# A linear-attention and FFN layer on one core: TensorE visits later code, and the first batch is rearranged

## The reference

```python
x = x + attn(layernorm(x))                      # x: 32 x 512 x 256, float32
x = x + ffn(layernorm(x))                       # ffn adds its own input and a second layernorm
# attn: 16 heads of 16 features, phi = elu + 1, chunks of 128 rows, causal inside a chunk
q, k, v = phi(x @ Wq.T + bq), phi(x @ Wk.T + bk), x @ Wv.T + bv
scores = where(tril, q @ k.T, 0)
num = scores @ v + q @ S                        # S: sum of k.T @ v over earlier chunks
den = sum(q * (cumsum(k) + z))                  # z: sum of k over earlier chunks
attn = (num / den) @ Wo.T + bo
# ffn: both weights come as integers, minus 128, times a scale per group of 128 rows
ffn = x + 0.5 * (silu((layernorm(x) * gamma + beta) @ w1 + b1) @ w2 + b2)
```

## Time and profile before

| | us |
|---|---|
| median of 3 runs (lowest, highest) | 1394.21 (1392.43, 1395.14) |
| the profiled execution: time, span | 1391.56, 1389.8 |
| TensorE busy (weight load) | 1362.6 (1227.8) |
| VectorE, ScalarE, GpSimd busy | 1188.4, 1072.2, 659.1 |
| TensorE's share of the chain that ended last | 94% |

### The profile page before, as it was taken

One profiled execution on the slowest core, in us unless ns is written; L12 is line 12 of the kernel. 1 busy time (PEld: TensorE's weight loads), 2 busy tenths in 40 slices (PEclk: granted clock), 3 DMA queues, 4 the chain that ended last, 5 costly groups with the idle time before them and its releaser, 6 DMA issues.

```text
span 1389.8 us, 60917 instructions
## 1 busy us (share of the span) xinstructions
PE 1362.6 (98%) x25658; PEld 1227.8 (88%) x25658; DVE 1188.4 (86%) x1954; ACT 1072.2 (77%) x1754; POOL 659.1 (47%) x506
## 2 busy tenths in 40 slices
PE   6889999999999999999999999999999999999998
PEld 5778899988999988999988999888999889999887
DVE  7778888889888888888889888889888898888876
ACT  4668778888778887778887778887788887788863
POOL 3354443545444545444544445544535454445454
PEclk9899999999999999999999999999999999999999
DMA  6121211222211122212212212212112212112110
GB/s 180 43 48 45 60 41 50 53 53 45 60 38 53 45 57 48 59 36 55 45 45 60 47 45 58 45 45 60 43 48 53 53 45 60 39 51 49 42 31 31
DMA packets 93525, 71.89 MB, mean 52 GB/s; under 512 B 8768, under 2 KB 92992, under 8 KB 93504
## 3 DMA queue, kind: packets, MB, share of 16 engines
q1 hardware_dynamic: 92144, 71.59, 20.8%
q10 hardware_dynamic: 1360, 0.01, 0.1%
HBM read 38.03 MB, written 16.78 MB: 39 GB/s over the span
## 4 chain that ended last, share of the span: by engine, by line
PE 94%; DVE 2%; ACT 1%; issue 1%; DMA 1%; POOL 0%; SPq 0%; POOLq 0%; DVEq 0%; ACTq 0%
PE sc L308 25%; PE ring L308 19%; PE num L479 7%; PE num L308 6%; PE sc L449 5%; PE sc L370 5%; PE sc L371 5%; PE num L493 4%; PE ring L370 4%; PE ring L371 3%; PE ring L462 2%; PE num L352 2%; PE ring L435 2%; PE sc L343 1%; PE num L371 1%; PE num L370 1%
## 5 line engine op out<-in xcount | busy, mean ns | idle before, releaser
L1151 POOL TENSOR_TENSOR s_lo<-silu_f,s_hi 128x512 fp32r<-128x512 f32 x252 | 325.2, 1295 | 454.4 <-ACT s_hi L960 454.2
L953 ACT ACTIVATE silu_f<-silu_f 128x512 f32<-128x512 f32 x252 | 157.8, 626 | 28.1 <-DVE silu_f L691 27.2
L699 DVE TENSOR_TENSOR probs<-sc,causal 128x1024 f32<-128x1024 f32 x128 | 150.7, 1218 | 15.4 <-PE sc L449 12.5
L960 ACT ACTIVATE s_hi<-silu_f 128x512 fp32r<-128x512 f32 x252 | 153.7, 621 | 1.3
L1179 POOL TENSOR_TENSOR ln_rstd<-ln_in,minus_half 128x8 f32<-128x8 f32 x32 | 52.6, 1644 | 189.8 <-DVE ln_in L792 189.8
L308 PE MATMUL sc<-w_hi,s_hi 128*128 128x256 f32 x488 | 137.2, 281 | 0.0
L308 PE MATMUL sc<-w_hi,s_lo 128*128 128x256 f32 x488 | 137.1, 281 | 0.0
L308 PE MATMUL sc<-w_lo,s_hi 128*128 128x256 f32 x488 | 137.1, 281 | 0.0
L946 ACT ACTIVATE silu_f<-ring,bias,scale 128x512 f32<-128x512 f32 x93 | 72.4, 779 | 83.3 <-PE ring L371 79.3
L308 PE MATMUL ring<-w_lo,s_hi 128*128 128x256 f32 x480 | 134.9, 281 | 0.0
L308 PE MATMUL ring<-w_hi,s_lo 128*128 128x256 f32 x480 | 134.9, 281 | 0.0
(11 more groups left out here) (198 smaller groups left out, 4320.0 us busy)
## 6 DMA issues: line engine op xcount, KB each, us to landing
x_in<-in_x SPq DMA_DIRECT2D x32, 512.0 KB, 5.0
xb<-in_x SPq DMA_DIRECT2D x32, 512.0 KB, 3.4
rb<-den_rows SPq DMA_DIRECT2D x256, 64.0 KB
out<-out_t SPq DMA_DIRECT2D x64, 256.0 KB, 2.2
probs<-in_q SPq DMA_DIRECT2D x2, 512.0 KB, 8.8
silu_f<-in_q SPq DMA_DIRECT2D x2, 512.0 KB, 7.6
res<-in_sc SPq DMA_DIRECT2D x1, 512.0 KB, 7.4
out_t<-in_sc SPq DMA_DIRECT2D x1, 512.0 KB, 9.0
```

The lines of the kernel that those rows point to most:

```text
L699: masked.done(e.tensor_tensor(probs[:, t, 2 * h:2 * h + 2, :, :, :].rearrange("p g m a q -> p (g m a) q"), sc[:, 2 * h:2 * h + 2, :].rearr ...
L953: silu.done(e.activation(slot(j, A), slot(j, A), ACT.Silu))
L960: sh.done(e.activation(s_hi[:, j, :], slot(j, A), ACT.Copy))
L1151: sl.done(e.tensor_tensor(s_lo[:, j, :], slot(j, A), s_hi[:, j, :].bitcast(F32), ALU.subtract))
```

## The change

TensorE gets four landings, places that hold one empty instruction and a jump back. `visit` jumps to one and comes back; `landing_here` places it inside other code, which jumps over it. `values_landing` (between `values(0)` and `values(1)`) and `states_landing` (between `from_states(0)` and `from_states(1)`) are in the first batch and visited from the preparation. `second_landing` (behind `fc1(3)`) and `third_landing` (behind `fc1(6)`) are in the loop and visited from the first batch. The loop itself never visits them.

Around them, in preparation and first batch: the values' projection of batch 0 goes to banks 0 and 1, `w_q` is made by GpSimd, VectorE takes the statistics of the next input ahead of the features, the reciprocals come behind the second mask and `x_hat` behind the fourth, the small vectors for beta and their sum are placed elsewhere, with their products in the bank of `den`, the cumulations come ahead of `bias_1` and `x_hat`, and `q_by_parity` for batch 1 goes from ScalarE to GpSimd.

```diff
-        SPARE = 0
+        SPARE = (0, 1)
...
+        def v_bank(n, i):
+            return bank(SPARE[n]) if isinstance(i, int) and i < 0 else use_bank(f"v{n}")
...
-                            if (0 <= w.i + shift < B) if earlier else other in present:
+                            if earlier and w.i + shift == 0 and other in ("v0", "v1"):
+                                pass
+                            elif (0 <= w.i + shift < B) if earlier else other in present:
                                 takers.append((k, event, shift))
                                 break
                         else:
...
                     n += 1
             return last
-        def pe_tokens(e, w, n, lhs, use, present, event):
-            free_bank(w, use, present)
+        def pe_tokens(e, n, lhs, use, target, event):
             for h in range(2):
                 toks = slice((2 * int(use[-1]) + h) * P, (2 * int(use[-1]) + h + 1) * P)
-                last = pe_split3(e, use_bank(use)[:, h * D:(h + 1) * D], [
+                last = pe_split3(e, target[:, h * D:(h + 1) * D], [
                     ((lhs[0][:, t, toks], lhs[1][:, t, toks]), (w_hi[n][:, t, :], w_lo[n][:, t, :])) for t in range(T)])
             event.done(last)
+        outside = {}
+        def visit(e, landing):
+            e.br(landing)
+            outside[landing] = nc.switch_bb(f"{landing}_back").parent
+        def landing_here(e, landing):
+            e.br(f"{landing}_over")
+            with nc.body(landing, parent=outside[landing], valid_engines=[e.engine]):
+                e.nop()
+                e.br(f"{landing}_back")
+            nc.switch_bb(f"{landing}_over")
         def pe_iteration(e, i, A, Fn, N, N2, preparation=None):
             w = Waiter(e, i)
...
+                visit(e, "values_landing")
                 for c in range(C):
                     if c < C - 1:
                         e.wait_ge(p_xhat, c + 1)
...
+                pe_tokens(e, "v", (xt_hi, xt_lo), f"v{n}", v_bank(n, i), v_pe)
             def output_projection(n):
                 w.need(at_l)
-                pe_tokens(e, w, "o", attention_parts(N), f"wo{n}", present, wo_pe)
+                free_bank(w, f"wo{n}", present)
+                pe_tokens(e, "o", attention_parts(N), f"wo{n}", use_bank(f"wo{n}"), wo_pe)
             if not A and N:
                 first_transposes()
...
                     project_kq(n)
+                visit(e, "states_landing")
                 preparation["v"]()
+                preparation["values"]()
                 project_v(0)
                 project_v(1)
                 return
...
+                landing_here(e, "values_landing")
                 values(1)
                 x_transposes(0)
                 x_transposes(1)
                 from_states(0)
+                landing_here(e, "states_landing")
                 from_states(1)
                 project_kq(0)
                 project_kq(1)
                 project_kq(2)
+                visit(e, "second_landing")
                 preparation["o"]()
                 output_projection(0)
                 output_projection(1)
                 project_kq(3)
                 project_v(0)
                 project_v(1)
-                w.need(e_x1, 0, 0)
+                visit(e, "third_landing")
+                w.need(phi, 1, 0)
                 preparation["bias_1"]()
                 return
             if not A:
...
             values(0)
             fc1(2)
             fc1(3)
+            landing_here(e, "second_landing")
             fc1(4)
             values(1)
             from_states(0)
             x_transposes(1)
             fc1(5)
             fc1(6)
+            landing_here(e, "third_landing")
             fc1(7)
             with e.If(i != B - 1):
...
+                ve_norm_x(e, w, 2)
                 features(0)
                 features(1)
                 cumulate(0)
                 features(2)
                 features(3)
                 cumulate(1)
-                preparation["w1"]()
-                ve_norm_x(e, w, 2)
                 return
             if A and not Fn:
                 mask(*MASK_ORDER[0])
+                mask(*MASK_ORDER[1])
                 reciprocals()
-                mask(*MASK_ORDER[1])
-                ve_x_hat(e, w, 1)
+                preparation["w1"]()
                 mask(*MASK_ORDER[2])
                 mask(*MASK_ORDER[3])
+                ve_x_hat(e, w, 1)
                 sum_states()
-                preparation["biases"]()
+                preparation["parts"]()
                 input_lo(0)
                 input_lo(1)
                 preparation["o"]()
                 add_residual(1)
                 norm_x1()
                 ve_norm_x(e, w, 2)
+                preparation["beta"]()
                 norm_factors()
                 features(2)
                 features(3)
+                cumulate(0)
+                cumulate(1)
                 preparation["bias_1"]()
                 ve_x_hat(e, w, 2)
-                cumulate(0)
-                cumulate(1)
                 return
             if not A:
                 ffn_input_lo(0)
...
+                        v_bank(n, i)[toks, :].rearrange("p (c a x) -> p c a x", a=2, x=HD), ACT.Copy)
                 v_sb.done(last)
             def ffn_norm():
                 preparation["w2"]()
                 exponential(3)
                 values_out(0)
+                values_out(1)
                 ffn_norm()
-                values_out(1)
-                q_by_parity(0)
                 table_silu()
-                q_by_parity(1)
                 return
             if not N:
                 ffn_input_hi(0)
...
+                w.need(phi, 1, 2 * t + 1)
+                w.need(sc_pe, 0, t)
+                for odd in range(2):
+                    last = e.tensor_scalar(q_mask[:, t, odd, :], phi_q[:, t, :], parity[:, odd:odd + 1], None, ALU.mult)
+                q_par.done(last)
             def ln2_factors():
                 if not A:
                     return
             if A and not Fn:
                 input_bias()
+                q_by_parity(0)
                 ln2_factors()
                 po_norm(e, w, 2)
+                q_by_parity(1)
                 query_sums(0)
                 query_sums(1)
                 preparation()
         block = ctx.enter_context(nc.Block())
         WORDER = "kqvo"
-        V_QK, V_BIAS_O, V_W1, V_PARTS, V_W2, V_BETA = 2, 3, 4, 7, 8, 10
+        V_QK, V_BIAS_O, V_PARTS, V_W2, V_BETA = 2, 3, 5, 7, 9
         PAR = 6
         def stage_of(n):
...
+            for t in range(T):
+                e.tensor_scalar(w1_q[:, t, :], w1_i[t], -128.0, None, ALU.add).then_inc(p_w1, 1)
+            po_norm(e, Waiter(e, -1), 2)
             po_iteration(e, -1, False, False, True, False)
-            po_norm(e, Waiter(e, -1), 2)
             e.wait_ge(p_v, V_BIAS_O)
             def weights_2_lo():
...
-                e.wait_ge(p_wdma["1"], 16 * T)
-                for t in range(T):
-                    last = e.tensor_scalar(w1_q[:, t, :], w1_i[t], -128.0, None, ALU.add)
-                last.then_inc(p_v, 1)
-                e.wait_ge(p_v, V_W1)
-            def biases():
-                e.wait_ge(p_late, 16 * 4)
-                e.tensor_scalar(bias_2[:, :], bias_2[:, :], 0.5, None, ALU.mult).then_inc(p_v, 1)
+                e.tensor_tensor(bias_o[:, :], bank(SPARE[0])[:, 0:D], bias_o[:, :], ALU.add).then_inc(p_v, 1)
+            ve_iteration(e, -1, False, False, True, True, {"kq": projections, "v": values_weights})
+            e.wait_ge(p_par, PAR + 2)
+            def weights_2(n):
+                e.wait_ge(p_wdma["2"], 16 * 4)
+                e.scalar_tensor_tensor(out=w2_f[n], in0=w2_i[n], scalar=-128.0, in1=w2_f[n], op0=ALU.add, op1=ALU.mult)\
+                    .then_inc(p_v, 1)
+            def sums_of_beta():
+                e.wait_ge(p_pe, 2)
+                e.tensor_reduce(out=beta_w1[:, :, :], in_=use_bank("den")[:, 0:2 * T * FT].rearrange("p (t j a) -> p t j a", t=T, a=2),
+                                op=ALU.add, axis=mybir.AxisListType.X).then_inc(p_v, 1)
+            def parts_of_beta():
+                e.wait_ge(p_dma, 16 * 4)
                 e.tensor_scalar(beta_parts[:, :, 0], beta_c[:, :], 1.0, None, ALU.mult).then_inc(p_v, 1)
                 e.wait_ge(p_v, V_PARTS - 1)
                 e.tensor_tensor(beta_parts[:, :, 1], beta_c[:, :], beta_parts[:, :, 0].bitcast(F32), ALU.subtract)\
                     .then_inc(p_v, 1)
-            ve_iteration(e, -1, False, False, True, True, {"kq": projections, "v": values_weights, "w1": weights_1})
-            e.wait_ge(p_par, PAR + 2)
-            def weights_2(n):
-                e.wait_ge(p_wdma["2"], 16 * 4)
-                e.scalar_tensor_tensor(out=w2_f[n], in0=w2_i[n], scalar=-128.0, in1=w2_f[n], op0=ALU.add, op1=ALU.mult)\
-                    .then_inc(p_v, 1)
+                e.wait_ge(p_late, 16 * 4)
```

(52 more changed lines are left out.)

6 lines of the change are left out of this document (removed).

## The result

| | median, us | lowest to highest | runs |
|---|---|---|---|
| before | 1395.07 | 1389.62 to 1398.17 | 20 |
| after | 1399.42 | 1391.79 to 1404.17 | 20 |

The ratio is 1.0031, 95% interval 1.0018 to 1.0043: slower, where 1387.0 and faster were forecast. The profiled execution took 1403.04 us, span 1401.3. It lies near the slow end of its 20 runs, while the profiled one of before lies in the faster half of its own. So the difference of the two spans, 11.5 us, is larger than that of the medians, 4.35, and profiles are used here for where time goes, ratios for how much.

A forecast was written before the change was run, and what follows sets the result against it. TensorE bounds the loop, so only time before about 90 us can be won: 2.4 + 3.9 + 0.8 = 7.1 us, giving 1384.5 profiled and a 1387.0 median (own range 1385 to 1389.5; eight in ten 1383 to 1391.5).

The forecast's parts named there:

- What bounds the kernel: Loop: TensorE busy 42.00 of 42.00 us, so the change can only win before about 90 us.
- The landings in the loop: Loop's first pass: blocks fetched ahead by visits stay loaded, removing stalls of 1.23, 0.82 and 1.84 us; taken 3.9.
- jumps buy nothing: Rival, chance 0.20: the landing's block is gone or not kept when its turn comes; 3.2 us gained, 1391.0.
- The visits themselves: First batch: visits to second_landing (hidden) and third_landing (queued matmuls against a 2.5 us fetch); bounds 0 and 2.5, taken 0.
- The rival of 0.06: Only current and next block kept after a jump: each visit fetches twice, 2.5 us exposed at third landing; 1393.5, chance 0.06.
- The two landings of the first batch: First batch's values(1): they remove the 0.62 us stall, counted as nothing since the first batch then waits for something else.
- The first batch rearranged: First batch: earlier scores, masks and reciprocals, with GpSimd taking work; first FFN matmul at 61.4, 2.4 us earlier.
- VectorE as the gate of `gt_lo`: Before the first FFN matmul: VectorE reaches gt_lo 5.7 us after hn_add, at 60.2; ScalarE needs at most 5.0.
- the stand before the output projection: First batch: TensorE stands 3.3 us until gt_lo is ready; the clock then falls, costing 1.6 us, hn_add at 54.5.
- The clock of the first FFN matmuls: First FFN matmuls: the stand before them shrinks to 1.7 us, so the clock may stay up; 0 or 1.6, taken 0.8.
- The rule against this change: Skill's instruction fetch: two lines held, taken branches fetch their target first, so each visit would lose; given little weight.
- the order: First batch and preparation rearranged, with the clock of the first FFN matmuls: 2.4 + 0.8 = 3.2 us gained.

The follow-up runs named there:

- e2: The kernel before with the four visits and landings (and two helpers) added and nothing else; ratio to before 1.0037 (1.0021 to 1.0053).
- e1: The kernel after with all visits and landings taken out, the rearranged preparation and first batch kept; ratio to before 0.9983 (0.9967 to 0.9999).
- e5: e1 with one visit, to second_landing behind fc1(3), from behind project_kq(2); run once, 1388.77 us.
- e8: e1 with one visit to second_landing, made inside from_states(0) behind its 20th matmul; run once, 1392.24 us.
- e11: e1 with norm_factors, bias_1 and x_hat ahead of the cumulations and the second masked pair on ScalarE; ratio to before 0.9958 (0.9944 to 0.9972).
- e6: e1 with two visits in a row from behind project_kq(2), to two landings side by side behind fc1(3); run once, 1384.80 us.
- e7: e1 with one visit, from behind project_kq(0) to a landing between project_v(0) and project_v(1), in the next block; run once, 1390.70 us.

## Why the prediction was wrong

**What bounds the kernel** was right: nearly all that changed lies before the second pass, and the loop's two new jumps cost at most 0.04 us in 28 passes.

**The landings in the loop** is the first step that failed. "If that leaves the blocks loaded, 1.23 and 1.84 us go", with 3.9 taken, rested on an inference from the loop: seven blocks stay, so eight may be held, so a block fetched ahead stays too. The stalls at both places are there in the kernel after and in e2, and all twelve blocks are fetched again in their turn. The loop's rows show that code once run in sequence is kept; they say nothing of code fetched out of sequence. Of the 3.89 us, 3.53 are left in the kernel after; the missing stall in `values(1)` is the open point at the end of the experiments. By itself this would still have left a faster kernel: the rival "jumps buy nothing" had 0.20, and 1391.0, 0.23% below before; e1, which has no visits to pay for, is 0.17% below.

**The visits themselves**, taken 0 with a bound of 2.5, is the second failed step, and the one that settled the sign: visits and landings together cost some 6.7 us (e1 to the kernel after), with whatever they save in the loop already taken off. `second_landing` was hidden in the kernel after, as forecast. `third_landing` cost 2.59 us, the bound, and more: the small products behind it ran at 3.54 instead of 1.84 us, since the clock fell. And I had given the two visits of the preparation no price at all. The first costs 4.53 us (6.26 in e2): its packet starts only 1.9 us after the warm-up has ended, while the weights are being loaded, and nothing is behind it in the queue. The rival of 0.06, in which each visit fetches twice and the third landing exposes 2.5 us, had the mechanism right in both points. At 1393.5 it was still too low, since it, too, gave the preparation's visits no price.

**The two landings of the first batch**, counted as nothing, did bring nothing, but not for the reason given. In e1, as in most of the runs, TensorE, not the DMA of the reciprocals, sets the attention's start, and the stalls in `values`, 0.94 and 2.35 us in e1, are exposed; in e5, where they are 0.57 and 1.25, the DMA sets it. The kernel before has 0.62 there; it also has waits of 3.24 and 1.13 us for `probs` around them, in which a fetch can pass unseen.

**The first batch rearranged** was right in its sum and in part of its mechanism: 2.4 + 0.8 = 3.2 us forecast, e1 measured 0.17% (2.4 us; interval 0.1 to 4.6), and 4.0 in the profile. VectorE as the gate of `gt_lo` was right. That `gt_lo` came 0.3 us from the forecast was partly luck, as two errors cancelled. `hn_add` came 0.9 us before the 54.5 taken, since neither the stand before the output projection nor the slow clock behind it occurred. From there to `gt_lo` VectorE needed 6.8 us instead of 5.7: beside the masked copies on GpSimd `x_hat` took 2.31 us instead of 1.38. The clock of the first FFN matmuls stayed at 1.00 in e1 (61.2 to 64.7 us), so this term was worth 1.6 and not the 0.8 taken.

**The rule against this change** deserved more than the little weight it got. Each visit to a block not held brought its packets and, where little was queued, a stand: 4.53 and 2.59 us in the kernel after, 4.75 in e8. The Trainium skill ("Runtime: NRT & Kernel Launch", Instruction fetch mechanics) says that a taken branch out of the current window waits for its target; the visits to blocks not held agree. Its sentence that only two lines are held would have the loop fetch in each pass, and no instruction packet shows between 125 and 1300 us. But the same section gives TensorE 128 KiB, refilled in blocks of 16, which is room for eight, and the seven blocks of the loop fit. So the loop's rows spoke only against two lines on TensorE. I took them as a reason to set the sentence on taken branches aside, too, and nothing in the rows had spoken against that one.

Terms put right: the forecast of 7.1 us faster loses the 3.9 for the landings, 6.7 for visits and landings as measured and 0.8 for the order (2.4 instead of 3.2), which is 4.3 slower; the medians say 4.35. These terms were taken from e1 and the kernel after, so they have to agree. The independent sum, 0.37% lost in e2 and 0.17% saved in e1, gives 0.20% or 2.8 us slower, against 0.31% measured with an interval from 0.18%.

## What to carry to other kernels

Count code as a transfer: in these runs a visit to code that isn't held cost two packets and a stand of TensorE between none and 6.3 us, depending on what was queued and what else was being loaded. Having been there did not keep the code; in the loop the straight way did. Before giving work to GpSimd, look which of VectorE's small SBUF operations will run beside its two-input ones: order them ahead, as in e11. And where the profile shows that something is kept, ask under which order it got there before building on it.

## What the runs showed of the hardware

- A visit to a block not held brings two packets of about 16 KB, and the pair is fetched again when the straight way comes to it (20, 16 and 14 packets with four, two and one such visits, 12 without).
- A second visit directly behind the first brings none (e6: 14), nor does a visit to the next block (e7: 12).
- The loop's code, seven blocks by the prediction's count, is not fetched again: no instruction packet on queue 8 from 125 to 1300 us in any run.
- TensorE's clock: behind the 2.59 us stand of the kernel after the granted clock was 0.50 from 62.4 to 72.6 us, the 1.2 GHz level, and the small products took 3.54 us instead of 1.84. In the kernel before it was 0.51 from 64.0 to 67.5 us, behind a stand of 2.66. But e5 has a stand of 2.54 us before the same FFN matmuls and then 1.00 (61.85 to 65.4 us), and e11 one of 1.84 and then 0.50: the length of the stand alone does not tell.
- VectorE's operations of 8 elements a partition took up to 2.27 us beside GpSimd's two-input ones, 0.17 without. GpSimd's took 2.1 instead of 1.3 us when a cumulation of VectorE had begun first.
